# A recurrence's input stage written anew: Newton steps per four units, normalise on GpSimd, twelve x buffers

## Chip, cores and metric

One core of a Trainium2 chip. The metric is the device time of one launch in microseconds (us), lower is better.

## The reference, cut to what matters

The model has four layers on x of 256 x 256 positions with 64 channels: a triangle-like conv layer, a recurrence, a second conv layer and a mixture of experts, each with a residual. The change touches the inputs of the recurrence:

```python
def _L0_ffn_ref(x, W, V, gamma, beta):      # x is already layer-normed over its 64 channels (_ln_t, eps 1e-5)
    Wx = jnp.einsum('bti,hi->bth', x, W)
    flat = Wx.reshape(B * T, H)
    mean = jnp.mean(flat, axis=0)
    var = jnp.var(flat, axis=0)
    Wx = ((flat - mean) * jax.lax.rsqrt(var + BN_EPS) * gamma + beta).reshape(B, T, H)
    Vt = V.T
    def step(yt, wx_t):
        yt = jax.nn.sigmoid(wx_t + yt @ Vt)
        return (yt, yt)
```

So each of the 65,536 positions is divided by its own standard deviation, multiplied by W (the mean over channels is taken out by folding it into W), and the statistics of the results over all positions give a scale and a shift.

## The kernel before

The program runs its stages one after the other, with a barrier of all engines between them: conv_project (tiles cp) and conv_combine (cc) of layer 0, scan_input (si), scan (sc), the two conv stages again, and experts (ex). P is 128 partitions, N is 256, C is 64 channels, H = 2 halves, R = 4 rows in a unit, G = 64 units. Only scan_input (L955) changes.

scan_input first zeroes the weight on VectorE, loads W twice into the diagonal blocks and gamma and beta twice each by six small loads (L984 to L990), and calls center_weights (L95), which builds the centering matrix by memsets, multiplies and copies back; each is a block of its own that ends in a barrier. Then comes the main block. For a unit u of 128 x 512 values:

- SP loads x into one of 4 buffers (L1007) once unit u-4 has been normalised.
- VectorE takes statistics in four instructions (measure, L242), makes the variance (L248), multiplies x by rstd (rescale, L1029) and, once wx is written, takes the statistics of the results (count, L1035). In its order, unit by unit: rescale(u+1), measure(u+3), count(u), variance of u+3.
- GpSimd raises 128x8 variances to the power -0.5 (find_scales, L257).
- TensorE transposes the normalised unit (flip, L1093, four transposes) into one of two banks tp and multiplies it by the weight (L1104, one product of 512 columns, seen in the trace as two records) into one of two banks po. Its order: product(u), flip(u+1).
- ScalarE copies tp to zt (take, L1120) and po to wx (L1127). Its order: wx of u, then take(u+1).

wx is one resident tile of 128 KB per partition. quads (L267) runs 60 units in a hardware loop of four and the last four straight. At the end VectorE aggregates (L1054), TensorE averages the two halves with the matrix average, and a few small instructions on VectorE and one power on GpSimd (L1086) give scale and shift.

conv_project already uses another way to rstd, which the change copies. VectorE makes a first guess by shift and subtraction on integers for four units at once (L505 to L511), and GpSimd runs three Newton steps of four small instructions on 128x32 (go, L558):

```python
go(y2, was, was, ALU.mult, 4 * k)
go(y2, y2, hv, ALU.mult, 4 * k + 1)
go(y2, y2, numbers[:, 2:3].to_broadcast([P, 4 * T]), ALU.subtract, 4 * k + 2)
go(y, was, y2, ALU.mult, 4 * k + 3)
```

## Time and profile before

| | us |
|---|---|
| median of 3 runs | 2231.13 (2226.07 to 2234.45) |
| profiled execution, its own time | 2233.01 |
| its span, first to last instruction | 2231.2 |
| TensorE busy in the span | 1686.2 (76%) |
| VectorE | 1549.5 (69%) |
| GpSimd | 1249.8 (56%) |
| ScalarE | 1179.3 (53%) |

The rows come from this one execution. Times are from the span's start. PE is TensorE's matmul side, PEld its weight loads, DVE VectorE, ACT ScalarE, POOL GpSimd, SP SyncE, and a q behind a name the engine's issuing side. L1093 is line 1093 of the kernel. A line of the timeline gives start, length, engine, line and operation; in brackets stands how long the engine had been idle and what ended that. Neighbouring instructions of one kind are merged (x4). A row of windows has the stretch, its length, the busy us (and instructions) of PE, PEld, DVE, ACT and POOL, TensorE's granted clock as a share of 2.4 GHz, the DMA engines' busy share and GB/s. A group row has busy us and mean ns, then idle time before it and what ended it. Shares of busy time are averages over all stages; this stage lasts under a tenth of the span.

### The profile page before, as it was taken

What the parts mean: (1) busy time and instruction counts of PE and PEld (TensorE: products, weight loads), DVE (VectorE), ACT (ScalarE), POOL (GpSimd) and SP (SyncE); (2) the same over time, 40 slices, a digit from 0 to 9 for tenths busy, and PEclk for the clock granted to TensorE, in tenths of its full rate; (3) what the DMA queues carried; (4) which work ended last, traced back from release to release, by engine and by line L of the source; (5) the groups of instructions that cost most, each with busy time, mean ns of one, the idle gap of its engine ahead of it and who ended that gap; (6) DMA issues with size and microseconds to landing.
All of it is one profiled execution on the core that took longest, in us unless ns stands there. A gap on an engine that the chain in (4) does not pass through costs nothing. (4 is left out here: it accounts for less than half of the span.)

```text
span 2231.2 us, 44386 instructions
## 1 busy us (share of the span) xinstructions
PE 1686.2 (76%) x11740; PEld 1127.2 (51%) x11740; DVE 1549.5 (69%) x4941; ACT 1179.3 (53%) x2674; POOL 1249.8 (56%) x1658
## 2 busy tenths in 40 slices
PE   5878838898736667947787873888774699999997
PEld 2444437787622226834444442777763444444442
DVE  6888712665657777856877872266566599999996
ACT  5898813333215556935766772333321666666651
POOL 5787703776767770005655660276676566666652
PEclk9999969999879998977999996999988599999999
DMA  3777647988753330976888874698876666666652
GB/s 113 203 189 195 171 117 204 302 292 269 236 166 89 94 89 1 189 170 203 250 255 246 234 213 114 197 304 281 271 237 194 160 181 186 187 181 186 183 153 81
DMA packets 475473, 423.18 MB, mean 190 GB/s; under 512 B 224690, under 2 KB 372402, under 8 KB 475314
## 3 DMA queue, kind: packets, MB, share of 16 engines
q1 hardware_dynamic: 402610, 303.87, 49.2%
q10 hardware_dynamic: 72704, 117.47, 15.7%
q8 instruction: 66, 1.08, 0.2%
q14 instruction: 93, 0.76, 0.1%
HBM read 236.68 MB, written 150.99 MB: 174 GB/s over the span
## 5 line engine op out<-in xcount | busy, mean ns | idle before, releaser
L699 PE MATMUL cp_pv<-cp_weight,cp_zt 64*128 64x320 f32 x2048 | 368.7, 468 | 102.5 <-ACT cp_zt L637 87.7
L257 POOL TENSOR_TENSOR cc_ln_rstd<-cc_ln_var,numbers 128x8 f32<-128x8 f32 x128 | 255.4, 1996 | 190.5 <-DVE cc_ln_var L248 181.4
L523 DVE SCALAR_TENSOR_TENSOR a_res<-cp_pv,cp_mask,cp_sig 128x64 f32<-128x64 f32 x1024 | 263.8, 322 | 127.6 <-ACT cp_sig L646 123.2
L829 PE MATMUL cc_sum<-a_res,cc_bch 128*128 (+1 forms) x2048 | 301.8, 297 | 65.2 <-DMA cc_bch<-b_scratch 62.3
L919 ACT ACTIVATE cc_p<-cc_sum 128x512 f32 (+1 forms) x128 | 135.9, 1062 | 384.1 <-PE cc_sum L829 258.8
L1540 DVE TENSOR_TENSOR ex_xe<-ex_spread,ex_xd 128x512 f32<-128x512 f32 x512 | 317.6, 683 | 21.3 <-PE ex_spread L1791 18.5
L646 ACT ACTIVATE cp_sig<-cp_pv 128x384 f32<-128x384 f32 x512 | 249.7, 493 | 128.9 <-PE cp_pv L699 126.6
L829 PEld LDWEIGHTS cc_sum<-a_res,cc_bch 128*128 128x128 f32 x2048 | 272.1, 206 | 88.7 <-issue 77.1
L699 PEld LDWEIGHTS cp_pv<-cp_weight,cp_zt 64*128 64x128 f32 x2048 | 183.8, 189 | 221.9 <-issue 193.2
L1807 PE MATMUL ex_po<-ex_xe,ex_expert 128*64 128x512 f32 x1024 | 250.6, 611 | 0.0
L897 POOL TENSOR_TENSOR cc_p<-cc_p,cc_g 128x512 f32 (+1 forms) x128 | 163.7, 1279 | 113.2 <-DVE cc_g L878 86.9
L626 ACT ACTIVATE cp_xn<-cp_x,cp_lift,cp_rstd 128x64 f32<-128x64 f32 x512 | 196.2, 438 | 53.3 <-POOL cp_lift L574 53.3
L242 DVE BATCH_NORM_STATS2 cc_ln_stats<-cc_p 128x6 f32 (+1 forms) x512 | 112.0, 281 | 133.3 <-ACT cc_p L919 133.0
L878 DVE TENSOR_TENSOR cc_g<-cc_po,cc_g 128x512 f32<-128x512 f32 x128 | 88.2, 689 | 161.2 <-PE cc_po L847 127.2
L1662 ACT ACTIVATE ex_xn<-ex_x,ex_lift,ex_rstd 128x64 f32<-128x64 f32 x512 | 181.9, 429 | 22.7 <-POOL ex_lift L1584 22.7
L601 POOL TENSOR_TENSOR cp_b_stage<-cp_b_stage,cp_mask 128x256 f32<-128x256 f32 x256 | 151.7, 614 | 59.8 <-DVE cp_b_stage L525 59.4
L1630 POOL TENSOR_TENSOR ex_rest<-ex_turned,ex_rest 128x512 f32<-128x512 f32 x64 | 81.8, 1278 | 173.3 <-ACT ex_turned L1722 173.3
L257 POOL TENSOR_TENSOR si_ln_rstd<-si_ln_var,numbers 128x8 f32<-128x8 f32 x64 | 127.9, 1999 | 65.6 <-DVE si_ln_var L248 65.6
L847 PEld LDWEIGHTS cc_po<-cc_weight,cc_pt 128*128 128x128 f32 x1024 | 146.4, 206 | 5.3
L924 ACT ACTIVATE cc_pt<-cc_tp 128x512 f32<-128x512 f32 x128 | 78.8, 615 | 130.7 <-PE cc_tp L837 116.2
L847 PE MATMUL cc_po<-cc_weight,cc_pt 128*128 128x128 f32 x1024 | 146.1, 290 | 0.0
L525 DVE TENSOR_TENSOR cp_b_stage<-cp_pv,cp_sig 128x128 f32<-128x128 f32 x512 | 144.0, 281 | 0.0
(187 smaller groups left out, 2991.8 us busy)
## 6 DMA issues: line engine op xcount, KB each, us to landing
cc_bch<-b_scratch SPq DMA_DIRECT2D x256, 256.0 KB, 3.9
gate_scratch<-cp_sig SPq DMA_DIRECT2D x128, 256.0 KB, 2.6
b_scratch<-cp_b_stage SPq DMA_DIRECT2D x128, 256.0 KB, 3.9
cc_g<-gate_scratch ACTq DMA_DIRECT2D x128, 256.0 KB, 4.4
after_conv<-cc_p ACTq DMA_DIRECT2D x128, 256.0 KB, 3.9
ex_xd<-ex_xt SPq DMA_DIRECT2D x256, 128.0 KB, 2.6
cp_x<-in_x SPq DMA_DIRECT2D x64, 256.0 KB, 3.3
cc_p<-in_x ACTq DMA_DIRECT2D x64, 256.0 KB, 3.5
```

The costliest lines, as they stand in the source:

```text
L257: pool.tensor_tensor(rstd[q][:], var[q][:], numbers[:, 0:1].to_broadcast([P, tiles]), ALU.pow).then_inc(scaled if shifts else known, 1)
L523: dve.scalar_tensor_tensor(a_res[:, h, :, row], bank[:, h, 3 * C:4 * C], mask_sb[:, h, row:row + 1], sig[u.mod(2)][:, 0, h, i, :], ALU.mul ...
L601: ins = pool.tensor_tensor(at, at, over(mask_sb[:, h, row_block(u)], CH).unsqueeze(1) .to_broadcast([P, CHUNKS, R, CH]), ALU.mult)
L626: ins = act.activation(xn[u.mod(2)][:, i, 0, :], xs[u.mod(8)][:, 0, i, :], ACT.Identity, scale=rstd[q][:, k, i * H:i * H + 1], bias=lift[q ...
L646: act.activation(sig[u.mod(2)][:, :, :, i, :].rearrange("p k h c -> p h k c"), pv[slot(u, i)][:, :, 0:3 * C].rearrange("p h (k c) -> p h k ...
L699: pe.matmul(pv[slot(u, i)][:, h, 0:COLS], zt[u.mod(2)][half, i * P:(i + 1) * P], weight[half, :], start=True, stop=True).then_inc(v_made, 1)
L829: ins = pe.matmul(psum[q][:, at:at + TI], bch[buf][:, k, :, c], a_res[:, k, bass.ds(s * SC + j * CH + c, 1), ih * TI:(ih + 1) * TI], start ...
L847: ins = pe.matmul(po[q][:, j * 2 * C:(j + 1) * 2 * C], pt[:, j * P:(j + 1) * P], weight[:], start=False, stop=True, skip_group_check=True)
L897: pool.tensor_tensor(at, at, gs[q][:], ALU.add).then_inc(added, 1)
L1540: dve.tensor_tensor(xe[u.mod(2)][:, :, h, i * P:(i + 1) * P], pb[k][:].rearrange("p (e t) -> p e t", e=EP), xd[u.mod(8)][:, h, i * P:(i + ...
L1662: ins = act.activation(xn[u.mod(2)][:, i, h, :], xs[u.mod(8)][:, h, i, :], ACT.Identity, scale=rstd[q][:, t:t + 1], bias=lift[q][:, t:t + 1])
L1807: ins = pe.matmul(po[h * HALF:(h + 1) * HALF, :], expert[:, e, :], xe[u.mod(2)][:, e, h, :], start=e == 0, stop=e == EP - 1)
```

## The change

- The six loads, the memset and center_weights are gone. The host packs the centering matrix, W in blocks, the averaging matrix, gamma and beta into one array; SP loads it as its fifth load, TensorE multiplies, and VectorE copies the folded weight once (fold).
- There is one block. SP asks for x at once, into 12 buffers instead of 4; unit u-12 must have been normalised.
- VectorE measures, makes a first guess for four units at once (first_guess) and counts unit s-9. It no longer normalises (ON_DVE is 0).
- GpSimd runs 12 Newton instructions per four units (newton) and then four normalises of 128x512 into 4 xn buffers instead of 2.
- TensorE flips u before the product of u-1, with three po banks instead of two. ScalarE takes zt of u before wx of u-1.
- All engines run straight code instead of a hardware loop.

The diff, cut: the larger removed parts, which are the function printed above, are left out, and the small statistics at the end, which differ in semaphore counts alone.

```diff
-def scan_input(nc, tag, x, w_t, gamma, beta, wx, scale, shift, ident, numbers):
+def newton(pool, numbers, guess, half_var, root, rstd, done, base):
+    three_halves = numbers[:, 2:3].to_broadcast(list(rstd.shape))
+    for k in range(3):
+        was = guess if k == 0 else rstd
+        for j, (out, a, b, op) in enumerate([(root, was, was, ALU.mult), (root, root, half_var, ALU.mult),
+                                             (root, root, three_halves, ALU.subtract), (rstd, was, root, ALU.mult)]):
+            if j or k:
+                pool.wait_ge(done, base + 4 * k + j)
+            pool.tensor_tensor(out, a, b, op).then_inc(done, 1)
+def scan_input(nc, tag, x, packed, wx, scale, shift, ident, numbers):
+    T = H * R
+    FOURS = G // 4
+    ROOTS = 12
+    NX = 12
...
+    ON_DVE = 0
...
-        xs = [m.sb(f"x{q}", [P, H, R, C]) for q in range(4)]
-        xn = [m.sb(f"xn{q}", [P, R, H, C]) for q in range(2)]
+        xs = [m.sb(f"x{q}", [P, H, R, C]) for q in range(NX)]
+        xn = [m.sb(f"xn{q}", [P, R, H, C]) for q in range(4)]
         zt = [m.sb(f"zt{q}", [P, R * P]) for q in range(2)]
-        find_variances, find_scales, rstd, known, (take_stats, finish_variances) = layer_norm(m, H * R, PLAIN, numbers)
+        stats = [m.sb(f"stats{q}", [P, 4, T, 3]) for q in range(2)]
+        half_var = m.sb("half_var", [P, 4 * T])
+        shifted = m.sb("shifted", [P, 4 * T], I32)
+        guess = m.sb("guess", [P, 4 * T], I32)
+        root = m.sb("root", [P, 4 * T])
+        rstd = [m.sb(f"rstd{q}", [P, 4, T]) for q in range(2)]
         batch = m.sb("batch", [P, G, 6])
...
-        po = [m.ps(f"po{q}") for q in range(2)]
+        po = [m.ps(f"po{q}") for q in range(3)]
...
+        def on_dve(u):
+            return u % 4 >= 4 - ON_DVE
+        def normalised(eng, u):
+            if on_dve(u):
+                eng.wait_ge(xn_dve, u // 4 * ON_DVE + u % 4 - (4 - ON_DVE) + 1)
+            else:
+                eng.wait_ge(xn_pool, u // 4 * (4 - ON_DVE) + u % 4 + 1)
+        def normalise(eng, u):
+            eng.wait_ge(refined, (u // 4 + 1) * ROOTS)
+            if u >= 4:
+                eng.wait_ge(xt_made, u - 3)
+            return eng.tensor_tensor(xn[u % 4][:], xs[u % NX][:].rearrange("p h i c -> p i h c"),
+                                     over(rstd[u // 4 % 2][:, u % 4, :].rearrange("p (i h) -> p i h", h=H), C), ALU.mult)
         with nc.Block() as block:
             @block.sync
             def _(sp):
...
+                for u in range(G):
+                    if u == 4:
+                        sp.dma_start(pack[:], packed).then_inc(loaded, 16)
+                    if u >= NX:
+                        normalised(sp, u - NX)
+                    sp.dma_start(xs[u % NX][:], x[:, :, u * R:(u + 1) * R, :]).then_inc(x_in[u % NX], 16)
             @block.vector
             def _(dve):
...
+                def measure(u):
+                    if u >= G:
+                        return
+                    q = u // 4 % 2
+                    dve.wait_ge(x_in[u % NX], (u // NX + 1) * 16)
+                    if u >= 8:
+                        dve.wait_ge(guessed, (u // 4 - 2) * 3 + 1)
+                    for i in range(R):
+                        ins = dve.bn_stats(stats[q][:, u % 4, i * H:(i + 1) * H, :].rearrange("p t s -> p (t s)"),
+                                           xs[u % NX][:, :, i, :].rearrange("p h c -> p c h"))
+                    ins.then_inc(counted, 1)
+                    if u % 4 == 3:
+                        first_guess(u // 4)
+                def first_guess(four):
+                    dve.wait_ge(counted, four * 4 + 4)
+                    if four:
+                        dve.wait_ge(refined, four * ROOTS)
+                    dve.tensor_scalar(half_var[:].rearrange("p (u t) -> p u t", t=T), stats[four % 2][:, :, :, 2], 0.5 / C,
+                                      0.5e-5, ALU.mult, ALU.add).then_inc(guessed, 1)
+                    dve.wait_ge(guessed, four * 3 + 1)
+                    dve.tensor_scalar(shifted[:], half_var[:].bitcast(I32), 1, None, ALU.logical_shift_right
+                                      ).then_inc(guessed, 1)
+                    dve.wait_ge(guessed, four * 3 + 2)
+                    dve.tensor_scalar(guess[:], shifted[:], -1, MAGIC, ALU.mult, ALU.add).then_inc(guessed, 1)
                 def count(u):
...
+                    if 0 <= u < G:
+                        dve.wait_ge(wx_made, u + 1)
+                        dve.bn_stats(batch[:, u, :], wx[:, :, u * R:(u + 1) * R]).then_inc(batched, 1)
+                def fold():
+                    dve.wait_ge(folded, 1)
+                    dve.tensor_copy(weight[:], po[0][:, 0:P]).then_inc(weight_made, 1)
+                for s in range(G + LATE):
+                    measure(s)
+                    if s == 3:
+                        fold()
+                    for u in range(4 * (s // 4) - 4, 4 * (s // 4)):
+                        if s % 4 == 2 and 0 <= u < G and on_dve(u):
+                            normalise(dve, u).then_inc(xn_dve, 1)
+                    count(s - LATE)
...
             @block.gpsimd
             def _(pool):
...
+                for four in range(FOURS):
+                    pool.wait_ge(guessed, four * 3 + 3)
+                    if ON_DVE and four >= 2:
+                        pool.wait_ge(xn_dve, (four - 1) * ON_DVE)
+                    newton(pool, numbers, guess[:].bitcast(F32), half_var[:], root[:],
+                           rstd[four % 2][:].rearrange("p u t -> p (u t)"), refined, four * ROOTS)
+                    for u in range(four * 4, four * 4 + 4 - ON_DVE):
+                        normalise(pool, u).then_inc(xn_pool, 1)
+                pool.wait_ge(end, 6)
                 pool.tensor_tensor(inv[:], inv[:], numbers[:, 0:1], ALU.pow).then_inc(inv_made, 1)
             @block.tensor
             def _(pe):
-                def flip(n, q):
-                    pe.wait_ge(xn_made, n + 5)
+                def flip(u):
+                    normalised(pe, u)
+                    if u >= 2:
+                        pe.wait_ge(zt_made, u - 1)
                     for i in range(R):
-                        ins = pe.transpose(tp[q][:, i * P:(i + 1) * P], xn[q][:, i].rearrange("p h c -> p (h c)"),
+                        ins = pe.transpose(tp[u % 2][:, i * P:(i + 1) * P], xn[u % 4][:, i].rearrange("p h c -> p (h c)"),
                                            ident[:])
                     ins.then_inc(xt_made, 1)
-                flip(0, 0)
-                pe.wait_ge(w_in, 16 * 3 * H)
-                def unit(u, t, j, ahead):
-                    q = j % 2
+                def product(u):
                     pe.wait_ge(zt_made, u + 1)
...
+                    if u >= 3:
+                        pe.wait_ge(wx_made, u - 2)
+                    pe.matmul(po[u % 3][:], weight[:], zt[u % 2][:], start=True, stop=True).then_inc(o_made, 1)
+                pe.wait_ge(loaded, 16)
+                pe.matmul(po[0][:, 0:P], center, blocks, start=True, stop=True).then_inc(folded, 1)
+                flip(0)
+                pe.wait_ge(weight_made, 1)
+                for u in range(1, G):
+                    flip(u)
+                    product(u - 1)
+                product(G - 1)
+                pe.wait_ge(end, 1)
+                pe.matmul(pm[:, 0:2], average, moments[:], start=True, stop=True).then_inc(averaged, 1)
+                pe.wait_ge(end, 5)
+                pe.matmul(pm2[:, 0:1], average, var[:], start=True, stop=True).then_inc(averaged, 1)
             @block.scalar
             def _(act):
...
+                def take(u):
+                    act.wait_ge(xt_made, u + 1)
+                    if u >= 2:
+                        act.wait_ge(o_made, u - 1)
+                    act.activation(zt[u % 2][:], tp[u % 2][:], ACT.Copy).then_inc(zt_made, 1)
+                def take_wx(u):
                     act.wait_ge(o_made, u + 1)
-                    act.activation(wx[:, :, bass.ds(u * R, R)].rearrange("p s i -> p i s"),
-                                   po[q][:].rearrange("p (i s) -> p i s", i=R), ACT.Copy).then_inc(wx_made, 1)
-                    if ahead:
-                        take(u + 1, 1 - q)
-                quads(act, unit)
+                    act.activation(wx[:, :, u * R:(u + 1) * R].rearrange("p s i -> p i s"),
+                                   po[u % 3][:].rearrange("p (i s) -> p i s", i=R), ACT.Copy).then_inc(wx_made, 1)
+                take(0)
+                for u in range(1, G):
+                    take(u)
+                    take_wx(u - 1)
+                take_wx(G - 1)
...
+def pack_scan(w_in, gamma, beta):
+    eye = np.eye(H, dtype=np.float32)
+    ones = np.ones((H, H), np.float32)
+    small = np.eye(C, dtype=np.float32)
+    packed = np.zeros((P, 3 * P + 2), np.float32)
+    packed[:, 0:P] = np.kron(eye, small - np.float32(1.0 / C))
+    packed[0:C, P:P + C] = w_in.T
+    packed[C:P, P + C:2 * P] = w_in.T
+    packed[:, 2 * P:3 * P] = np.kron(0.5 * ones, small)
+    packed[:, 3 * P] = np.tile(gamma, 2)
+    packed[:, 3 * P + 1] = np.tile(beta, 2)
+    return packed
```

## Rows read from the trace of the kernel before

**Rows 1.** Windows of the inputs' stage; busy us and instruction counts per engine.

```profile
661.00:842.00 181.00, 113.83 (x383) 46.79 (x384) 137.96 (x447) 92.75 (x127) 127.93 (x64) 0.98 0.31 91
```

**Rows 2.** Timeline, start of the stage (start us, length us, engine, line).

```profile
648.25 0.17 DVE L994 MEMSET si_weight<- 128x128 f32 x1 [4.45 <-PEq L58]
...
658.11 13.91 SPq L1007 DMA_DIRECT2D si_x<-after_conv  x7
...
661.13 0.88 DVE L242 BATCH_NORM_STATS2 si_ln_stats<-si_x 128x6 f32<-128x128 f32 x4 [2.54 <-DMA si_x<-after_conv]
...
663.98 0.69 DVE L1029 TENSOR_TENSOR si_xn<-si_x,si_ln_rstd 128x512 f32<-128x512 f32 x1 [0.51 <-POOL si_ln_rstd L257]
```

**Rows 3.** Timeline, two steady units of the stage.

```profile
745.96 0.88 DVE L242 BATCH_NORM_STATS2 si_ln_stats<-si_x 128x6 f32<-128x128 f32 x4
...
746.10 0.66 PE L1093 MATMUL si_tp<-ident,si_xn 128*128 128x128 f32 x4
746.24 1.03 ACT L1127 ACTIVATE wx<-si_po 128x512 f32 x1 [1.31 <-PE si_po L1104]
747.08 0.62 ACT L1120 ACTIVATE si_zt<-si_tp 128x512 f32<-128x512 f32 x1
747.45 0.69 DVE L1035 BATCH_NORM_STATS2 si_batch<-wx  x1 [0.61 <-ACT wx L1127]
...
747.75 1.13 PE L1104 MATMUL si_po<-si_zt,si_weight 128*128 128x512 f32 x2 [1.00 <-ACT si_zt L1120]
...
749.01 1.04 ACT L1127 ACTIVATE wx<-si_po 128x512 f32 x1 [1.31 <-PE si_po L1104]
```

**Rows 4.** Waits in the stage: engine line, waited for, us in total, times, longest.

```profile
PE si_po L1104 <- ACT si_zt L1120: 62.6, 64, 1.1
```

**Rows 5.** Timeline, the stage's last unit.

```profile
839.11 0.67 DVE L1029 TENSOR_TENSOR si_xn<-si_x,si_ln_rstd 128x512 f32<-128x512 f32 x1
...
843.84 0.69 DVE L1035 BATCH_NORM_STATS2 si_batch<-wx 128x6 f32<-128x512 f32 x1 [1.97 <-ACT wx L1127]
```

**Rows 6.** Timeline, start of the first conv stage.

```profile
8.46 17.40 SPq L428 DMA_DIRECT2D cp_x<-in_x  x10
...
15.98 0.18 DVE L505 TENSOR_SCALAR cp_half_var<-cp_stats 128x32 f32<-128x32 f32 x1
...
16.51 3.22 DVE L493 BATCH_NORM_STATS2 cp_stats<-cp_x 128x6 f32<-128x128 f32 x16
16.75 0.24 POOL L558 TENSOR_TENSOR cp_root<-cp_guess 128x32 f32<-128x32 f32 x1 [15.15 <-DVE cp_guess L511]
...
20.65 0.26 POOL L558 TENSOR_TENSOR cp_lift<-cp_stats,cp_rstd 128x32 f32<-128x32 f32 x1
```

**Rows 7.** Groups on GpSimd by shape, whole run.

```profile
L1630 POOL TENSOR_TENSOR ex_rest<-ex_turned,ex_rest 128x512 f32<-128x512 f32 x64 | 81.8, 1278 | 173.3 <-ACT ex_turned L1722 173.3
...
L1606 POOL TENSOR_TENSOR ex_below<-ex_below,ex_second 128x256 f32<-128x256 f32 x16 | 11.6, 726 | 1.3
```

**Rows 8.** Timeline of GpSimd, two neighbours in the last stage.

```profile
1899.15 1.28 POOL L1630 TENSOR_TENSOR ex_rest<-ex_turned,ex_rest 128x512 f32<-128x512 f32 x1 [2.40 <-ACT ex_turned L1722]
1900.39 1.65 POOL L1579 TENSOR_TENSOR ex_rstd<-ex_var,numbers 128x8 f32<-128x8 f32 x1
```

**Rows 9.** Windows, the recurrence's straight code.

```profile
870.00:920.00 50.00, 47.01 (x268) 41.18 (x268) 43.33 (x139) 44.32 (x134) 0.00 (x0) 0.93 0.51 103
```

**Rows 10.** Powers by tile: min/median/max ns, first and last start us.

```profile
L257 POOL TENSOR_TENSOR si_ln_rstd<-si_ln_var,numbers x64: 1635/2009/2131, 662.3 to 836.7; 128x8 f32<-128x8 f32 x64
```

**Rows 11.** Timeline of TensorE in the first combine stage.

```profile
581.69 0.66 PE L837 MATMUL cc_tp<-ident,cc_pn 128*128 128x128 f32 x4 [2.04 <-DVE cc_pn L871]
...
589.23 0.61 PE L844 MATMUL cc_po<-cc_bias,ones 128*128 128x512 bf16 x1 [3.58 <-ACT cc_pt L924]
```

**Rows 12.** Windows of 2 us around those two; PEclk is the granted clock.

```profile
582.00:584.00 2.00, 1.31 (x12) 1.05 (x10) 1.97 (x7) 0.60 (x1) 2.00 (x2) 1.00 0.29 56
...
588.00:590.00 2.00, 0.78 (x3) 0.69 (x4) 0.21 (x1) 0.60 (x1) 1.72 (x1) 0.50 0.69 206
```

123 lines of the change are left out of this document (23 added, 100 removed).

## The prediction

> **What bounds the kernel now.** The change touches one stage only, the one that makes the recurrence's inputs (tiles named si), so I first cut it out with the windows view. Its 64 units run from about 661 to 844 us, and in that stretch no engine is full: VectorE is busy 138 of 181 us, GpSimd 128, TensorE 114, ScalarE 93 [rows 1]. A stage where nobody is full is set by a ring of waits, or by a transfer. The list of waits says which: the product waits for ScalarE's zt in all 64 units [rows 4]. The timeline of two steady units shows the ring closed, for wx in its turn waited 1.31 us for the product [rows 3]. ScalarE starts wx of a unit at 746.24, zt of the next at 747.08 (it stands behind wx on the same engine), the product starts at 747.75 when zt is there, and wx follows it at 749.01 [rows 3]. That is 0.84 + 0.67 + 1.26 = 2.77 us for a unit. Everything else fits inside: VectorE's normalise (0.69), four statistics (0.88) and count (0.69), and GpSimd's power of 2.0 us, which the reader should see is long but waits for nobody's sake. Over the stage: first normalise at 663.98 [rows 2], last ending at 839.11 + 0.67 = 839.78 [rows 5], so 63 periods in 175.1 us, 2.78 each. The ring holds to the end.
>
> Before the ring there is a head. The stage's first instruction is at 648.25, but the first load of x is issued only at 658.11 and is measured at 661.13 [rows 2]. The 9.9 us between are six small weight loads, a fold of the weight in a block of its own, and two barriers.
>
> **The change, part by part.** Every step below refers to the code of the stage.
>
> *Head.* Weight loads, center_weights and both barriers go; SP issues x at once, from about 648.3. What the new head costs can be read from the first conv stage, which already does this work in the same shape: first load at 8.46, first guess at 15.98, Newton at 16.75 [rows 6]. So 8.29 us from the first load to Newton, with a mask load ahead of it in that stage that is absent here, and with four units measured first. That puts Newton of the first four at 648.3 + 8.3 = 656.6. Bounds: 1.5 us earlier without the mask, 2 us later, if the larger pack (fifth on SP's queue) and eleven x loads crowd the first ones. The fold (one product, one copy on VectorE after the fourth measurement) lies under Newton; with that cover gone it would cost under 2 us once. SP's waits hold nothing back: it asks for unit u when u-12 is normalised, so a load has eight units, where the one seen took 3.0 us [rows 2].
>
> *GpSimd, the new work.* Newton is 12 dependent products on 128x32. The first conv stage shows 12 such steps from 16.75 to 20.65 [rows 6], so 3.90 us per four units, where the powers took 4 x 2.0 = 8.0. Then four normalises of 128x512, two inputs, one of them in permuted order. The trace has this shape on GpSimd in the last stage: ex_rest, permuted in the same way, 1278 ns [rows 7], and the next independent instruction starts 1.24 us after it [rows 8]. So a four takes 3.90 + 4 x 1.24 = 8.86 us, 2.22 per unit. What could make a normalise dearer: the dearest GpSimd product per element is L1606 with 726 ns for 256 [rows 7], or 1.45 us for 512; a four is then 3.90 + 4 x 1.41 = 9.54. I take 1.24, since shape, type and permutation agree, and keep 9.54 for the range. I see no reason for less than 1.2, which would take 3 us off in all.
>
> *VectorE.* It loses the normalise and keeps 0.88 + 0.69 for a unit; the three operations of the guess take 0.77 once per four (15.98 to 16.75). 4 x 1.57 + 0.8 = 7.1 us per four, below 8.86. Its guess for the next four waits for Newton of this one (half_var and guess have one buffer), with count and measure of the units after it queued behind that wait; GpSimd needs the guess only after its four normalises, 4 x 1.24 = 5 us later. I followed the order: the count ahead of the fourth measurement becomes free about 8 us after Newton's end, so the next guess is ready some 10.5 us after it against a need at 8.9 + 5 = 13.9. Slack 3 us; this hides the guess.
>
> *TensorE and ScalarE.* The ring goes: PE now flips u before the product of u-1, and ScalarE takes zt of u before wx of u-1, with three po banks. So each engine counts by its own work: PE 0.66 + 1.13 = 1.8 us per unit, 7.2 per four; ScalarE 0.62 + 1.03, 6.6 per four. Both are below 8.86. A new wait: the product of a four's last unit now stands behind the flip of the next four's first, thus behind Newton; wx and count of that unit are late by it, and VectorE's slack above already counts this. The four xn buffers let GpSimd run a whole four ahead, so it never waits for a flip.
>
> *Tail.* Before, from the last normalise's end to the last count's end: 839.78 to 844.53, 4.75 us [rows 5]. Now the product of unit 62 comes in between, while zt and wx overlap it: 0.06 + 0.76 + 2 x 1.13 + 0.12 + 1.03 + 0.03 + 0.69 = 4.95. What follows (aggregate, averages, scale, shift) is as before: the averages and gamma were waiting ready anyway.
>
> *Straight code for the loop.* Costed at nothing: the recurrence after it is straight code already and PE issued 268 matmuls in 50 us there, 5.4 per us, busy 47 of 50 [rows 9]; here it needs 6 per 2.2 us.
>
> **Sum.** 656.6 + 16 x 8.86 = 798.4; + 5.0 = 803.4, where it was 844.5: 41 us less, of which 3 to 4 come from the head (first normalise at 660.5, not 663.98) and the rest from the period. The profiled execution took 2233.0 us around its span of 2231.2, so 2192; the median of the runs is 1.9 below it, so **2190 us**.
>
> **A rule against the change.** GpSimd's side: ex_rest takes 1278 ns where VectorE's normalise of the same size takes 0.69 us, 1.87 times as long [rows 2, 7]. The Trainium skill, GPSIMD Engine Reference, section 4.1, says to keep elementwise work with two inputs off GpSimd, where it is about twice as slow. By that rule the move should lose 64 x 0.6 us = 38 us of the one engine's time on the other, 2269 in all. By the rows it loses nothing, as VectorE's time was not what the ring was made of, and GpSimd gets 4 us back per four from the powers. I give the rule's outcome, as rival 4, 0.01.
>
> And the two engines disturb each other: GpSimd's power of the same shape takes 1635 ns at least and 2009 in the middle [rows 10]; the fast one, at the stage's start, had no VectorE normalise beside it. The Trainium skill, GPSIMD Engine Reference, section 1 (Specifications), says that its memory interfaces are shared with VectorE and that VectorE instructions with two memory inputs contend; the trace agrees, and after the change VectorE has none of these left in the loop.
>
> **Rivals.**
> 1. *GpSimd is stretched by VectorE's statistics.* They are busy 1.57 of 2.2 us per unit. For it: the 2009 against 1635. Against it: Newton in the first conv stage ran beside 16 statistics without slowing, 3.90 us for 12 steps [rows 6]. If a normalise gets the power's extra 0.37 us: 8.86 + 1.5 = 10.3 per four, 16 x 1.5 = 24 us back, 2214.
> 2. *The other side: TensorE falls to its lower level (1.2 GHz) and stays there.* The gap is now longer: idle about 8.9 - 7.2 = 1.7 us once per four, in place of two gaps of about 1 us a unit. At the lower level the same work takes about twice: 4 x 3.6 = 14.3 us per four, at most; PE, not GpSimd, becomes the bound, and 16 x (14.3 - 8.9) = 86 us are lost, 2276. Where the lower level holds for a part of the stage only, the point that decides is a mean of 11.4 us per four ((844.5 - 5.0 - 656.6) / 16), beyond which the kernel is slower. Against it: granted 1.00 still after an idle 2.04 us, and 0.50 only after one of 3.58 us with little work before it [rows 11, 12]. In this stage 0.98 was granted with PE busy 63% [rows 1], and it will now be 80%.
> 3. *Little changes:* the period stays near 2.75 us because some order that I followed wrongly closes a new ring (guess behind count behind wx behind the next flip, for instance), or straight code comes late. Then only the head is won, 3 to 5 us: 2227.
>
> **Chances.** Forecast 0.79, its own range 2182 to 2203 (the bounds above: head -1.5 and +2, period 8.7 to 9.54, and the runs' own spread of 4 us to each side); rival 1 0.09, rival 2 0.04, rival 3 0.07, rival 4 0.01. To leave out no more than 2 in 10 the range reaches into rival 1: 2182 to 2212. A measurement of this kernel tells about 0.5% (11 us) from no change. Forecast and rival 1 are faster by more; rival 3 is within; rivals 2 and 4 are slower: faster 0.88, same 0.07, slower 0.05.
>
> **What would show it.** GpSimd filled in the stage, with 12 steps of 0.325 us and four instructions of 1.28, fours 8.9 us apart; first normalise near 660.5, last count near 803; TensorE waiting once per four for GpSimd's normalise, granted clock near 1.0; ScalarE's waits for the product gone short; the guess never the releaser of Newton after the first four. The forecast is wrong if Newton waits for the guess, if normalise is over 1.3 us, if the granted clock falls, or if a wait on x appears after the first units.

## The result and the profile after

Four runs each: 2232.79 us before (2226.07 to 2236.63), 2173.94 after (2171.02 to 2176.92). The ratio is 0.974, 95% interval 0.9711 to 0.9768: faster by 59 us, where 41 were forecast. In later runs, six of the changed kernel and eleven of the one before on one chip, it was 2169.18 against 2224.51, ratio 0.9748 (0.9717 to 0.9779). The profiled execution took 2174.94 us around a span of 2172.5.

The stage first. Timeline of the changed kernel, its start:

```profile
644.86 2.59 SPq L1032 DMA_DIRECT2D si_x<-after_conv  x4
...
652.80 0.18 DVE L1059 TENSOR_SCALAR si_shifted<-si_half_var 128x32 int32<-128x32 int32 x1
...
653.28 0.24 POOL L964 TENSOR_TENSOR si_root<-si_guess 128x32 f32<-128x32 f32 x1 [11.43 <-DVE si_guess L1062]
...
657.15 4.04 POOL L1020 TENSOR_TENSOR si_xn<-si_x,si_rstd 128x512 f32<-128x512 f32 x4
657.19 1.04 DVE L1056 TENSOR_SCALAR si_half_var<-si_stats 128x32 f32<-128x32 f32 x1 [0.66 <-POOL si_rstd L964]
...
658.26 0.97 DVE L1059 TENSOR_SCALAR si_shifted<-si_half_var 128x32 int32<-128x32 int32 x1
659.26 0.97 DVE L1062 TENSOR_SCALAR si_guess<-si_shifted 128x32 int32<-128x32 int32 x1
```

From the first load to Newton are 8.42 us, and to the first normalise 12.29. GpSimd does the four normalises in 4.04 us, one starting every 1.00 us. The second guess falls beside them: its three instructions end at 658.23, 659.23 and 660.23, and the first three normalises at 658.20, 659.19 and 660.20.

The steady part, where [rows 3] showed the ring before. Timeline, one period of four units:

```profile
714.89 0.49 DVE L1056 TENSOR_SCALAR si_half_var<-si_stats 128x32 f32<-128x32 f32 x1
...
715.41 0.96 DVE L1059 TENSOR_SCALAR si_shifted<-si_half_var 128x32 int32<-128x32 int32 x1
...
716.41 0.97 DVE L1062 TENSOR_SCALAR si_guess<-si_shifted 128x32 int32<-128x32 int32 x1
...
717.46 0.24 POOL L964 TENSOR_TENSOR si_root<-si_guess 128x32 f32<-128x32 f32 x1
...
718.69 1.05 ACT L1154 ACTIVATE wx<-si_po 128x512 f32<-128x512 f32 x1
...
718.89 1.09 PE L1129 MATMUL si_po<-si_zt,si_weight 128*128 128x512 f32 x2
...
720.04 1.05 ACT L1154 ACTIVATE wx<-si_po 128x512 f32<-128x512 f32 x1
...
721.34 4.04 POOL L1020 TENSOR_TENSOR si_xn<-si_x,si_rstd 128x512 f32<-128x512 f32 x4
...
722.44 0.66 PE L1121 MATMUL si_tp<-ident,si_xn 128*128 128x128 f32 x4 [2.46 <-POOL si_xn L1020]
...
725.50 0.24 POOL L964 TENSOR_TENSOR si_root<-si_guess 128x32 f32<-128x32 f32 x1
```

Newton begins at 717.46 and again at 725.50: 8.04 us for four units, 2.01 each, against 2.78 before. GpSimd is all but full in it: 3.88 us of Newton, 4.04 of normalise, and 0.12 until it starts anew. TensorE stands still for 2.46 us once per four and then goes through the units 1.35 us apart (ScalarE's wx at 718.69 and 720.04). The guess ends at 717.38, 0.04 behind the last normalise (713.30 + 4.04) and 0.08 ahead of Newton. So the 0.12 are a short wait for the guess. It is there in 14 of the 15 fours after the first; in the other one the guess was ready 0.92 us early, and the period was 7.88 instead of 8.04.

The guess's two integer operations take 0.96 and 0.97 us, where the same operation took 0.18 at the stage's start, with GpSimd idle (652.80). They don't work for that long: after the first four, all 45 instructions of the guess end 0.04 us behind the end of a normalise, whatever their start. So each waits for the normalise that is running, and the engine is counted as busy meanwhile.

The windows view of 50 us in the stage (columns as in [rows 1]), to be read beside [rows 1]:

```profile
700.00:750.00 50.00, 38.49 (x149) 21.07 (x148) 49.35 (x141) 36.01 (x50) 43.47 (x100) 0.91 0.45 133
```

VectorE is busy 49.35 of 50 us, but some 1.9 of each 8.04 are that waiting inside the guess (0.49 + 0.96 + 0.97 against 3 x 0.18). GpSimd's 43.47 is the smaller number only because the 0.08 us between two dependent instructions isn't counted as busy. The granted clock is 0.91.

The waits between 650 and 800 us that answer to [rows 4]:

```profile
PE si_tp L1121 <- POOL si_xn L1020: 33.0, 16, 5.3
...
PE si_po L1129 <- ACT si_zt L1150: 0.2, 1, 0.2
```

The product's wait for zt went from 62.6 us in 64 waits to 0.2 in one. What TensorE waits for is now GpSimd's normalise, once per four. The end of the stage, to be read beside [rows 5]:

```profile
779.63 2.04 POOL L1020 TENSOR_TENSOR si_xn<-si_x,si_rstd 128x512 f32<-128x512 f32 x2
...
781.82 1.13 PE L1129 MATMUL si_po<-si_zt,si_weight 128*128 128x512 f32 x2
...
782.78 0.60 PE L1121 MATMUL si_tp<-ident,si_xn 128*128 128x128 f32 x4
...
786.77 0.69 DVE L1067 BATCH_NORM_STATS2 si_batch<-wx 128x6 f32<-128x512 f32 x1 [0.62 <-ACT wx L1154]
787.50 1.89 DVE L1083 BATCH_NORM_AGGREGATE si_moments<-si_batch 128x2 f32<-128x384 f32 x1
```

**The account.** GpSimd's last instruction of the stage ahead was at 643.88 before and at 640.58 after. From there to the last count's end: 200.65 us before, 787.46 - 640.58 = 146.88 after. So 53.8 of the 59 us are the stage. Of the others, 3.3 are an earlier arrival at it, and the rest of the kernel took 1385.0 against 1386.7. The other stages vary by some us between runs (what follows the stage takes 1374.4 to 1384.5 in the runs below), so experiments are compared by the length of the stage: from its first load of x to the aggregate of the counts. That is 844.56 - 658.11 = 186.45 before and 787.50 - 644.86 = 142.64 after. The 9.9 us of weight work ahead of the first load come on top of the gain.

### The profile page after: what moved, and what is told of

Same layout as the page of the kernel before. It is cut to its first block and busy times, and to the rows that moved or that the text cites. A ratio compares the mean times of both kernels' runs of the same rounds, so it can differ in the third digit from the quotient of the medians.

```text
span 2172.5 us, 43839 instructions
## 1 busy us (share of the span) xinstructions
PE 1663.2 (77%) x11740; PEld 1128.5 (52%) x11740; DVE 1536.1 (71%) x4852; ACT 1178.0 (54%) x2674; POOL 1232.1 (57%) x1850
## 3 DMA queue, kind: packets, MB, share of 16 engines
q8 instruction: 69, 1.13, 0.2%
## 5 line engine op out<-in xcount | busy, mean ns | idle before, releaser
L1569 DVE TENSOR_TENSOR ex_xe<-ex_spread,ex_xd 128x512 f32<-128x512 f32 x512 | 317.6, 683 | 21.2 <-PE ex_spread L1820 18.2
L626 ACT ACTIVATE cp_xn<-cp_x,cp_lift,cp_rstd 128x64 f32<-128x64 f32 x512 | 196.2, 438 | 53.8 <-POOL cp_lift L574 53.8
L1659 POOL TENSOR_TENSOR ex_rest<-ex_turned,ex_rest 128x512 f32<-128x512 f32 x64 | 81.7, 1277 | 173.1 <-ACT ex_turned L1751 173.1
L558 POOL TENSOR_TENSOR cp_root<-cp_guess 128x32 f32<-128x32 f32 x32 | 7.6, 238 | 236.7 <-DVE cp_guess L511 236.7
```

The costliest lines, as they stand in the source:

```text
L626: ins = act.activation(xn[u.mod(2)][:, i, 0, :], xs[u.mod(8)][:, 0, i, :], ACT.Identity, scale=rstd[q][:, k, i * H:i * H + 1], bias=lift[q ...
L1569: dve.tensor_tensor(xe[u.mod(2)][:, :, h, i * P:(i + 1) * P], pb[k][:].rearrange("p (e t) -> p e t", e=EP), xd[u.mod(8)][:, h, i * P:(i + ...
```

## The experiments

What is open: why a normalise took 1.04 us instead of 1.28, which part of the change gave how much, and what bounds the stage now. All times in one table; "before" is the kernel before on the same chip, one run of it, or the median of eleven where it is 2224.51. Single runs, except the last two rows (5 and 6 runs). Each stage time is from one profiled run; the changed kernel's two are 142.64 and 143.79, so that a difference of 1 or 2 us says nothing.

| run | kernel us | before us | stage us |
|---|---|---|---|
| full_operand | 2172.17 | 2218.89 | 144.06 |
| natural_read | 2173.73 | 2218.89 | 144.58 |
| old_order | 2206.32 | 2218.89 | 187.84 |
| x_buffers_8 | 2166.45 | 2218.89 | 144.45 |
| ones_operand | 2181.43 | 2236.11 | 155.1 |
| straight_before | 2219.87 | 2236.11 | 181.9 |
| power_per_four | 2192.27 | 2236.11 | 167.9 |
| normalise_on_dve | 2177.87 | 2236.11 | 151.7 |
| order_alone | 2381.59 | 2223.18 | 350.9 |
| one_on_dve | 2162.93 | 2223.18 | 141.66 |
| two_guess_buffers | 2157.54 | 2223.18 | 140.76 |
| two_newton_rounds | 2155.45 | 2224.51 | 125.29 |
| x_buffers_4 | 2260.16 | 2224.51 | 232.87 |
| newton_per_eight | 2148.03 | 2224.51 | 121.67 |
| changed_again | 2169.18 | 2224.51 | 143.79 |

**full_operand.** The second operand of the normalise is the x tile itself, in full. It leaves out the scaling by rstd.

```diff
-                                     over(rstd[...].rearrange("p (i h) -> p i h", h=H), C), ALU.mult)
+                                     xs[u % NX][:].rearrange("p h i c -> p i h c"), ALU.mult)
```

> GpSimd's normalise here takes x itself as second operand in place of the standard deviation's inverse, which is repeated 64 times along the innermost direction; shape, permutation, order and waits stay. It leaves the scaling by rstd out. Theory (the repeated operand makes it cheap: 1042 ns, where a full second operand costs 1278): a normalise takes about 1.27 us, a four 3.9 + 4 x 1.24 = 8.9 us in place of 8.04, 16 x 0.85 = 14 us more, about 2187. Rival (the permuted write and the write in place of ex_rest made that one dear): 1.04 us and 2174, unchanged.

The normalise took 1041 ns and the stage 144.06 us: nothing changed. "A full second operand is dear" fell, at least for one in the same tile as the first.

**natural_read.** x is read in the order in which it lies, and xn is written permuted.

```diff
-            return eng.tensor_tensor(xn[u % 4][:], xs[u % NX][:].rearrange("p h i c -> p i h c"),
-                                     over(rstd[...].rearrange("p (i h) -> p i h", h=H), C), ALU.mult)
+            return eng.tensor_tensor(xn[u % 4][:].rearrange("p i h c -> p h i c"), xs[u % NX][:],
+                                     over(rstd[...].rearrange("p (i h) -> p h i", h=H), C), ALU.mult)
```

> The same normalise on GpSimd, read in natural order and written permuted, as ex_rest is, with the repeated second operand kept. Theory (the repeated operand decides): 1.04 us each and 2174. Rival (the permuted write decides): 1.27 us each, about 2187.

1049 ns, 144.58 us. The order is not what makes the price.

**ones_operand.** The second operand is a full tile of ones, in its own memory, which VectorE fills once ahead of its first measurement. It too leaves out the scaling by rstd.

```diff
-                                     over(rstd[...].rearrange("p (i h) -> p i h", h=H), C), ALU.mult)
+                                     ones_x[:].rearrange("p h i c -> p i h c"), ALU.mult)
```

> GpSimd's normalise multiplies x by a separate full tile of ones, which is not x itself as in the run before; it leaves the scaling by rstd out. Theory (two different full operands make a GpSimd product dear, one that repeats or is the same tile does not): 1.27 us each, a four 8.9 us, 13 us more in the stage than the 142.6 us from first load to aggregate of the changed kernel, so about 156. Rival (the addition of ex_rest, or its writing in place, is what costs): 1.04 us and 143 us.

Its timeline, one period of GpSimd and the guess in it:

```profile
705.80 0.25 POOL L964 TENSOR_TENSOR si_root<-si_guess 128x32 f32<-128x32 f32 x1
...
709.69 4.95 POOL L1024 TENSOR_TENSOR si_xn<-si_x,si_ones_x 128x512 f32<-128x512 f32 x4
...
711.02 1.20 DVE L1063 TENSOR_SCALAR si_shifted<-si_half_var 128x32 int32<-128x32 int32 x1
...
714.60 0.24 POOL L964 TENSOR_TENSOR si_root<-si_guess 128x32 f32<-128x32 f32 x1
```

Four normalises take 4.95 us instead of 4.04, one 1270 ns, and the period is 8.80: the forecast's 8.86, found with the operand that the forecast's row has. So the form of the second operand is the cause: two different full tiles cost 1.27 us, a second operand that repeats along the innermost dimension, or the first operand's own tile, 1.04. The guess is stretched in step: its integer operations take 1.19 to 1.20 us here, as the normalise that they wait for starts every 1.23 us and no longer every 1.00.

**old_order.** The changed kernel with the order of before on TensorE and ScalarE.

```diff
                 for u in range(1, G):
+                    product(u - 1)
                     flip(u)
-                    product(u - 1)
...
                 for u in range(1, G):
+                    take_wx(u - 1)
                     take(u)
-                    take_wx(u - 1)
```

> The changed kernel with the old order on two engines: TensorE does the product of u-1 before the flip of u, ScalarE writes wx of u-1 before zt of u. Theory (the ring was the bound, and its opening is what let the rest show): a unit takes 2.77 us again, 64 x 2.77 = 177 us where the changed kernel takes 128, so about 2222. Rival (the earlier loads, later count and more buffers give the time by themselves, and the order is worth little): 2174 to 2180.

Its timeline, one unit and the start of the next:

```profile
717.22 1.13 PE L1129 MATMUL si_po<-si_zt,si_weight 128*128 128x512 f32 x2 [1.11 <-ACT si_zt L1150]
...
718.38 1.04 ACT L1154 ACTIVATE wx<-si_po 128x512 f32<-128x512 f32 x1 [1.22 <-PE si_po L1129]
...
719.22 0.63 ACT L1150 ACTIVATE si_zt<-si_tp 128x512 f32<-128x512 f32 x1
...
719.90 1.13 PE L1129 MATMUL si_po<-si_zt,si_weight 128*128 128x512 f32 x2 [1.12 <-ACT si_zt L1150]
...
721.06 1.03 ACT L1154 ACTIVATE wx<-si_po 128x512 f32<-128x512 f32 x1 [1.22 <-PE si_po L1129]
```

The ring is back, closed by the same three steps as in [rows 3]: wx 0.84, zt 0.68, product 1.16 from start to start, 2.68 us a unit. The stage is 187.84 us, 45.2 over the changed kernel and as long as before (186.45), although Newton, GpSimd's normalise and the buffers are all there. Of this kernel's whole time some 10 us came back in other stages.

**order_alone.** The reverse: the new order in the kernel before, in its loop, with two buffers each and the count not made later.

```diff
+                    if ahead:
+                        pe.wait_ge(zt_made, u + 1)
+                        flip(u + 1, 1 - q)
+                    pe.wait_ge(zt_made, u + 2)
                     pe.wait_ge(wx_made, u + 1)
                     pe.matmul(po[q][:], weight[:], zt[q][:], start=True, stop=True).then_inc(o_made, 1)
-                    if ahead:
-                        flip(u + 1, 1 - q)
...
+                    if ahead:
+                        take(u + 1, 1 - q)
+                    act.wait_ge(o_made, u + 2)
                     act.activation(wx[...], po[q][...], ACT.Copy).then_inc(wx_made, 1)
-                    if ahead:
-                        take(u + 1, 1 - q)
```

> The kernel before with the new order alone: flip of u+1 before the product of u, zt of u+1 before wx of u; four x buffers, powers, loop and VectorE's order (normalise of u+1, measure of u+3, count of u) as they were. Theory (the order needs the late count): count of u now waits for a product that stands behind the flip of u+1, and so behind VectorE's own normalise just ahead of it; the chain normalise, flip, product, wx, count is 0.69 + 0.78 + 1.25 + 1.08 + 0.61 = 4.4 us per unit, the stage from first load to aggregate about 285 us in place of 186.5, about 2330 in all. Rival (opening the ring is enough by itself, VectorE's 2.4 us then bound it): 160 us, 2205.

Its timeline, one unit:

```profile
747.36 0.69 DVE L1035 BATCH_NORM_STATS2 si_batch<-wx  x1 [2.93 <-ACT wx L1134]
...
748.04 0.68 DVE L1029 TENSOR_TENSOR si_xn<-si_x,si_ln_rstd 128x512 f32<-128x512 f32 x1
...
748.77 1.11 PE L1093 MATMUL si_tp<-ident,si_xn 128*128 128x128 f32 x4 [2.74 <-DVE si_xn L1029]
...
749.68 1.92 PE L1107 MATMUL si_po<-si_zt,si_weight 128*128 128x512 f32 x2
...
751.72 1.02 ACT L1134 ACTIVATE wx<-si_po 128x512 f32 x1 [1.12 <-PE si_po L1107]
752.92 0.69 DVE L1035 BATCH_NORM_STATS2 si_batch<-wx  x1 [3.41 <-ACT wx L1134]
```

5.56 us a unit, twice the time before. Here is a longer ring: count, then normalise behind it on VectorE, flip, product, wx, count. Expected were 4.4 us a unit. Most of the excess is TensorE, which in a window from 700 to 900 has a mean granted clock of 0.58, near its lower level (1.2 GHz), with 98 of 200 us busy: the flip takes 1.11 us instead of 0.66 and the product 1.92 instead of 1.13. So the new order is worth nothing without the late count (LATE is 9 in the changed kernel) and a normalise that no count holds back.

**straight_before.** The kernel before with its loops in the stage written out, nothing else.

```diff
-    with eng.Fori(0, G // 4 - 1) as t:
+    for t in range(G // 4 - 1):
...
-                with sp.Fori(0, G // 4) as t:
+                for t in range(G // 4):
```

> The kernel before with its hardware loops in this stage written out as straight code, nothing else. Theory (the loop costs a little in the ring: 2.77 us a unit in the loop, 2.68 in the straight run of the old order): 64 x 0.09 = 6 us less in the stage, from first load (658.1) to aggregate (844.6) 186.5 us before, so 180 to 181. Rival (code loading costs at least as much as the loop): 186 us or more.

The stage took 181.9 us instead of 186.45, wx starting every 2.68 us (746.15, 748.83, 751.50). So straight code is worth some 4.6 us to this ring, and 2.68 is what old_order has too. The kernel before shows it by itself: its last four units are straight code, and wx starts there at 837.44, 840.11 and 842.78, every 2.67 us.

**power_per_four.** The changed kernel with one power on 128x32 in place of twelve Newton instructions (the guess is still made, and its first instruction now gives the whole variance and not half of it).

```diff
-                    newton(pool, numbers, guess[:].bitcast(F32), half_var[:], root[:],
-                           rstd[four % 2][:].rearrange("p u t -> p (u t)"), refined, four * ROOTS)
+                    pool.tensor_tensor(rstd[four % 2][:].rearrange("p u t -> p (u t)"), half_var[:],
+                                       numbers[:, 0:1].to_broadcast([P, 4 * T]), ALU.pow).then_inc(refined, 1)
```

> The changed kernel with one power on 128x32 per four units in place of 12 Newton instructions (the guess is still made, unused). A power on 128x8 takes 1635 ns undisturbed where a product on 128x8 takes about 205, so 0.18 us per column: theory (time goes by columns): 0.2 + 32 x 0.18 = 5.9 us, 2 us more than Newton's 3.9 per four, the stage 16 x 2 = 32 us longer, 175 us from first load to aggregate. Rival (much of the power is a fixed cost): about 2.2 us, the four 6.3 us, until VectorE with 8 us per four bounds it: 140 to 143 us.

Groups on GpSimd in its stage (columns: busy us, mean ns, idle):

```profile
L1107 POOL TENSOR_TENSOR si_rstd<-si_half_var,numbers 128x32 f32<-128x32 f32 x16 | 86.7, 5417 | 11.5 <-DVE si_guess L1062 11.2
```

5.42 us against Newton's 3.90, and 16 x 1.5 = 24 us: the stage is 25.3 us longer, 7 less than expected.

**normalise_on_dve.** ON_DVE 4: VectorE normalises, GpSimd has Newton alone.

```diff
-    ON_DVE = 0
+    ON_DVE = 4
```

> All four normalises go back to VectorE (ON_DVE = 4), with the rest of the change kept. VectorE then has per four 4 x (0.79 + 0.60) of statistics, 4 x 0.6 to 0.69 of normalise and 0.6 of guess = 8.6 to 8.9 us, and GpSimd 3.9. Theory (VectorE becomes the bound, and the move to GpSimd was worth 0.6 to 0.9 us per four): 152 to 157 us from first load to aggregate, 142.6 in the changed kernel. Rival (waits between VectorE's order, Newton and TensorE make a chain of their own, since the normalises of a four stand together behind Newton): 10 us per four or more, 175 us.

151.7 us, 9.1 longer. Its waits:

```profile
POOL si_root L964 <- DVE si_guess L1062: 82.8, 16, 12.2
```

Here VectorE is the bound (39.59 of 40 us busy), and GpSimd waits for each guess. So moving the normalise is worth 9 us of the 44; the ring was opened without it.

**one_on_dve** (ON_DVE 1) and **two_guess_buffers** (ON_DVE 1, half_var and guess in two buffers each, LATE 13) asked whether the last unit of four is better on VectorE.

```diff
-    LATE = 9
+    LATE = 13
...
-    ON_DVE = 0
+    ON_DVE = 1
...
-        half_var = m.sb("half_var", [P, 4 * T])
+        half_vars = [m.sb(f"half_var{q}", [P, 4 * T]) for q in range(2)]
...
-                    if four:
-                        dve.wait_ge(refined, four * ROOTS)
...
+                    if four >= 2:
+                        dve.wait_ge(refined, (four - 1) * ROOTS)
```

> One of four normalises on VectorE (ON_DVE = 1), three on GpSimd. GpSimd's work falls from 8.0 to 7.0 us per four. VectorE has 5.6 us of statistics, 0.6 of normalise and 0.6 of guess undisturbed, 2.4 as stretched by GpSimd's normalises. Theory (VectorE is already full and the stretch stays): 8.1 to 8.6 us per four, 144 to 150 us from first load to aggregate, no gain over 142.6. Rival (the stretch goes when GpSimd has idle time): 7.0 to 7.3 us per four, 127 to 131 us.

> As one_on_dve, but half_var and guess have two buffers, so the guess of the next four need not wait for Newton of this one, and the count is 13 units late in place of 9. Theory (the guess moves to where Newton runs, beside short instructions, and takes 0.6 us): 7.0 to 7.3 us per four, 127 to 131 us from first load to aggregate and some 12 us less than the changed kernel. Rival (VectorE's place in the order still puts the guess beside a normalise): as one_on_dve, 144 to 150 us.

141.66 and 140.76 us, 1 to 3 us less than the 142.6 to 143.8 of the changed kernel, which a single run can't tell from nothing. Neither run did what was expected: not the 144 to 150 us of a full VectorE, nor the 127 to 131 of a guess that is out of the way. The timeline of two_guess_buffers shows why no more was won:

```profile
714.98 3.49 POOL L1020 TENSOR_TENSOR si_xn<-si_x,si_rstd 128x512 f32<-128x512 f32 x3
715.07 1.50 DVE L1020 TENSOR_TENSOR si_xn<-si_x,si_rstd 128x512 f32<-128x512 f32 x1
...
719.02 0.24 POOL L964 TENSOR_TENSOR si_root<-si_guess 128x32 f32<-128x32 f32 x1 [0.55 <-DVE si_guess L1063]
```

Beside GpSimd's normalise the same product takes VectorE 1.50 us, not the 0.69 of [rows 2]. GpSimd's three normalises take 3.49 us where three take 3.04 alone, and Newton then waits 0.55 for the guess. So of the 1.00 us that GpSimd is spared per four nearly all is lost again: the period is 7.93 us.

**x_buffers_8 and x_buffers_4**: NX = 8 and NX = 4 in the changed kernel.

```diff
-    NX = 12
+    NX = 8
```

> 8 x buffers in place of 12. A load is then asked for when the unit 8 earlier is normalised, which lies a whole four (8 us) ahead of the need, and a load takes 3 to 4 us: unchanged, 2174. Rival (VectorE is nearly full and needs its loads earlier): a wait on x at each four, some 1 to 2 us times 16, 2190 to 2206.

> 4 x buffers in place of 12. The loads of a four then start only when the same buffers of the four before are normalised, one each microsecond; the last lands 3 to 4 us after the last normalise, then its measure (0.9), the guess (0.6) and Newton (3.9), during which GpSimd normalises nothing: 4.0 + 3.5 + 0.9 + 0.6 + 3.9 = 12.9 us per four against 8.04, the stage 16 x 4.9 = 78 us longer, 220 us. The rival, that loads are quick enough: under 150 us.

Eight are as good as twelve (144.45 us). Four cost 90 us (232.87), as the next four can't be loaded, nor measured, before the last ones are normalised. The forecast of 12.9 us a four and 220 us was somewhat short: Newton starts every 13.7 to 14.4 us. Waits of x_buffers_4 between 650 and 800 us:

```profile
DVE si_stats L1045 <- DMA si_x<-after_conv: 87.7, 16, 8.5
```

**two_newton_rounds.** Eight Newton instructions for four units instead of twelve: rstd is coarser, and its sign is turned.

```diff
-    for k in range(3):
+    for k in range(2):
...
-    ROOTS = 12
+    ROOTS = 8
```

> The changed kernel with two rounds of Newton in place of three (8 instructions per four units, so a coarser inverse of the standard deviation). GpSimd's four falls from 8.04 to 3.9 x 2/3 + 4.1 = 6.7 us. If GpSimd is the bound alone, the stage gets 16 x 1.3 = 21 us shorter, 122 from first load to aggregate. If VectorE (busy 98.7% of the steady stretch, 2.4 us per four of it in the three stretched guess instructions) is as full as it looks, hardly anything is gained, 139 to 143. Between them: the guess is stretched less as GpSimd idles, and VectorE's own 5.5 + 0.7 to 1.5 us bound it at 6.7 to 7.2 us, 122 to 130.

The stage took 125.29 us, a period of 6.97 (713.21 to 720.18). GpSimd lost 1.3 us per four, the period 1.07; the rest shows as a wait. Its waits:

```profile
POOL si_root L964 <- DVE si_guess L1062: 16.4, 15, 11.5
```

16.4 us with the first wait of 11.5 taken off is 4.9 in 14, 0.35 each. VectorE is busy 49.28 of the 50 us from 700 to 750 there. So at 8.04 GpSimd is the bound, and at 6.97 VectorE is, with 0.8 us per four in which the guess's shift waits for a normalise.

**newton_per_eight.** Guess and Newton once per eight units, on 128x64, with NX 16 and LATE 17.

```diff
-    FOURS = G // 4
+    FOURS = G // 8
...
-    NX = 12
-    LATE = 9
+    NX = 16
+    LATE = 17
...
-        half_var = m.sb("half_var", [P, 4 * T])
+        half_var = m.sb("half_var", [P, 8 * T])
...
-                    if u % 4 == 3:
-                        first_guess(u // 4)
+                    if u % 8 == 7:
+                        first_guess(u // 8)
...
-                    for u in range(four * 4, four * 4 + 4 - ON_DVE):
+                    for u in range(four * 8, four * 8 + 8):
```

> Guess and Newton for eight units at once (128x64), 16 x buffers, the count 17 units late; all else as in the changed kernel. Newton's step goes by 0.325 us for 32 columns, and 1.6 ns a column more: 0.38 us for 64, 4.5 us per eight in place of 7.8. GpSimd per eight 4.5 + 8 x 1.0 = 12.6 us, VectorE 8 x 1.38 + 0.8 to 2.5 = 11.9 to 13.5. Theory (either bound falls by being paid half as often): 12.6 to 13.5 us per eight in place of 16.1, 8 x 3 = 24 us less in the periods, about 4 back at the start where eight units must be measured first: 122 to 128 us from first load to aggregate, about 2155. Rival (one of the two keeps it: VectorE's order blocks, or TensorE and ScalarE, which have bursts of eight, become late): 135 us or more.

> The changed kernel as it is, beside the run per eight on one chip, for the comparison: 142 to 145 us from first load to aggregate, 2165 to 2176 in all, and the same ratio to the kernel before.

Timeline of its GpSimd, one period of eight units:

```profile
711.70 8.05 POOL L1020 TENSOR_TENSOR si_xn<-si_x,si_rstd 128x512 f32<-128x512 f32 x8
719.88 0.29 POOL L964 TENSOR_TENSOR si_root<-si_guess 128x64 f32<-128x64 f32 x1
...
724.52 1.04 POOL L1020 TENSOR_TENSOR si_xn<-si_x,si_rstd 128x512 f32<-128x512 f32 x1
```

Its windows view:

```profile
700.00:740.00 40.00, 34.54 (x150) 19.55 (x151) 39.69 (x129) 34.28 (x49) 36.69 (x63) 1.00 0.52 158
```

12.82 us for eight units, 1.60 each instead of 2.01: twelve steps on 64 columns take 4.64 us, not twice 3.90. VectorE is full here as well, busy 39.69 of 40 us. The stage is 121.67 us, 22.1 shorter than changed_again's. The kernel takes 2148.03 us (2146.97 to 2151.29), ratio to before 0.9649 (0.9623 to 0.9675), and 21.2 us under the changed kernel on the same chip, 2169.18 (2161.73 to 2181.49). It beats both kernels.

## Why the prediction came out as it did

**The reading of before was right.** A ring of product, wx and zt set 2.77 us a unit; closed again in the changed kernel it gives the old stage back (187.84 against 186.45), and opened it gives 45 us.

**The head was right.** First load to Newton 8.42 us where 8.29 was read from [rows 6]; from the last GpSimd instruction ahead to the first normalise 20.10 before and 16.57 after, 3.5 less where 3 to 4 were said. The stage itself was reached 3.3 us earlier, which was not in the forecast. The fold is hidden: VectorE copies the folded weight at 653.11, 4 us ahead of the first normalise.

**Newton was right.** 3.88 us per four where 3.90 was read. That GpSimd would set the pace is shown by two_newton_rounds and ones_operand: with 1.3 us less of its work the period falls by 1.07, and with 0.91 more it grows by 0.76, up to 0.9 later in the stage.

**The step that failed is the price of a normalise**, "I take 1.24, since shape, type and permutation agree", and after it "I see no reason for less than 1.2". It measured 1.04, and four took 4.04 us instead of 4.96. With the small gaps the period was 8.04 instead of 8.86, 16 x 0.82 = 13 us, and from first load to last count the stage took 142.6 us, 12.5 less than the 155.1 of the forecast (803.4 - 648.3). This alone puts the time below the range. With the 3.3 us of the earlier arrival it makes up the distance from 2190 to 2173.94. The permutation had no part in it (natural_read). What counted, I had not compared: ex_rest adds two different full tiles, the normalise multiplies x by a scale that repeats along the innermost dimension. GpSimd's groups of the changed kernel, by form:

```profile
L1659 POOL TENSOR_TENSOR ex_rest<-ex_turned,ex_rest 128x512 f32<-128x512 f32 x64 | 81.7, 1277 | 173.1 <-ACT ex_turned L1751 173.1
L590 POOL TENSOR_TENSOR cp_xn<-cp_x,cp_rstd 128x256 f32<-128x256 f32 x128 | 78.7, 615 | 37.6 <-PE cp_tp L682 36.9
...
L1020 POOL TENSOR_TENSOR si_xn<-si_x,si_rstd 128x512 f32<-128x512 f32 x64 | 64.7, 1042 | 1.3
...
L558 POOL TENSOR_TENSOR cp_root<-cp_root,cp_half_var 128x32 f32<-128x32 f32 x96 | 24.2, 252 | 7.5
L558 POOL TENSOR_TENSOR cp_root<-cp_root,numbers 128x32 f32<-128x32 f32 x96 | 22.9, 239 | 7.5
...
L1638 POOL TENSOR_TENSOR ex_work<-ex_work,ex_pack 128x256 f32<-128x256 f32 x16 | 11.6, 727 | 1.0 <-DVE ex_work L1547 1.0
L1635 POOL TENSOR_TENSOR ex_below<-ex_below,ex_second 128x256 f32<-128x256 f32 x16 | 11.6, 725 | 1.3
...
L1627 POOL TENSOR_TENSOR ex_below<-ex_logit,ex_top 128x256 f32<-128x256 f32 x16 | 10.1, 630 | 11.0 <-DVE ex_top L1535 11.0
```

In the code, L590, L1627 and L558 with numbers have a second operand that repeats along the innermost dimension; L1635, L1659 and L558 with cp_half_var have a full one in another tile. L1638 has one that repeats, but along an outer dimension, and pays the price of a full one. All but L1020 were in the trace before as well (L590 with 617 ns, x128), and cp_xn is a normalise. From L558 with numbers and L590: (615 - 239) / 224 = 1.68 ns for a column beyond 32, so 239 + 480 x 1.68 = 1045 ns for 512, measured 1042. From L558 with cp_half_var and L1635: (725 - 252) / 224 = 2.11, so 1265, and ex_rest takes 1277. Both were there to be read, and the sum with the right row would have given 2190 - 13 = 2177. The "nearest row" had been chosen by shape, and the operand's form weighs more.

The Trainium skill, GPSIMD Engine Reference, section 3.1 (Elementwise — side-by-side cycle accounting), has one rate for two inputs, 4497 ns for 2048 elements, which would be an estimated 1124 ns here. The runs show two prices, on either side of it: 1042 and 1277 ns.

**VectorE's slack was wrong, and did not matter by luck.** Said were 7.1 us of work per four, a guess that is ready 10.5 us after Newton's end, and 3 us of slack. Three steps failed. The need was counted from the wrong four: the guess waits for Newton of the four ahead and is needed when that one's normalises are done, 4.1 us later, not 13.9. Had the 10.5 been right, Newton would have waited some 6 us in each four. But they were wrong too: the first instruction of the guess starts 1.7 us after Newton's end (714.89 against 713.22), as only a count and a measurement stand ahead of it. And the guess was priced at 0.77 us from a place where GpSimd did nothing; beside GpSimd's normalises it takes 2.49 us (714.89 to 717.38).

What it cost is small, as the last instruction of the guess just met the last normalise, waited for it and ended 0.04 us behind it. Newton did wait for it, which the forecast had named as a sign of being wrong, but for 0.16 us per four, the 8.04 against the 7.88 of the four in which the guess was early. In old_order GpSimd waits for flips, no normalise runs beside the guess (718.50 and 718.72, between the normalises at 716.26 and 718.93), and the two integer operations take 0.18 us again.

This answers to the sentence that the two engines' rule no longer applies as VectorE "has none of these left in the loop". The Trainium skill, GPSIMD Engine Reference, section 1 (Specifications), says that contention arises with VectorE instructions that have two memory inputs or run in a mode that uses both ports. The trace agrees for two inputs (VectorE's product 0.69 to 1.50 us in two_guess_buffers). The guess has one input and was stretched from 0.18 to 0.96, so the second half of the rule may be what it shows; in which mode it ran, no run here tells. The statistics (0.86 and 0.67 us) were not stretched, nor did they stretch GpSimd: every one of the 64 normalises took 1041 to 1044 ns. Rival 1 is thereby out.

**TensorE and ScalarE.** Each was to count by its own work, 1.8 and 1.65 us a unit. TensorE's burst runs at 1.35 us, since the flip overlaps the product, and its gap is 2.46 us once per four, not 1.7. It was right that neither is the bound. Rival 2 fell for this kernel: the clock in the window is 0.91, not near 1.0 as was said, but with no effect on the period. The rival's "about twice" at the lower level was more than order_alone then showed, 1.7 times (0.66 to 1.11 us, 1.13 to 1.92).

**The tail** was 787.46 - 781.67 = 5.8 us, not 4.95, 0.8 off against us. The term that failed is the 0.06 us from the last normalise to its flip: the flip starts at 782.78, 1.11 us after it. TensorE goes at 1.35 us a unit while GpSimd normalises one every 1.00, so it is behind at the end of a four and still has the product of unit 61 (781.82) ahead of the last flip. The counts behind it wait for ScalarE's wx (0.62 us at 786.77).

**The range** was added up unevenly: 2182 has the runs' spread of 4 us in it, 2203 (2190 + 2 + 11) has not. It would have been 2207, which changes neither the range as given, to 2212, nor the outcome.

**Straight code** was costed at nothing and was worth up to 4.6 us: that much in the kernel before. In the changed one a loop was not tried; its period is GpSimd's, so it may be worth less there.

**Where the gain is.** Each figure is what undoing one part alone costs the changed stage; they don't add up to 44: the order 45, four x buffers instead of twelve 90, the power instead of Newton 25, the normalise back on VectorE 9. Eight buffers would do. The third po bank, the four xn buffers and the late count were not undone one by one; that the late count is needed is argued from order_alone's ring.

## What to carry to other kernels

Price an instruction on GpSimd by a row whose operands have the same form (a second operand repeating, the same tile, or another full tile), before shape and order; the two differ by 0.23 us in 1.27. When a ring of waits is opened, ask of every engine left what it can do in the new period with its neighbours busy: VectorE's slack here went into instructions that waited for GpSimd's to end, not into work, and a busy share of 98.7% did not show it. And when short dependent steps set the pace, make them wider: 32 more columns cost 0.06 us a step, and Newton for eight units instead of four was worth another 21 us.
